# A fused cross-attention and expert FFN kernel: the opening loads cut into other groups, put in another order, and two of them held back

## What is computed

```python
# one layer
qh, kh, vh = heads(layernorm(x) @ wq + bq), heads(ctx @ wk + bk), heads(ctx @ wv + bv)   # 16 heads of 8
out = softmax((qh @ kh^T * 8**-0.5) @ vh, axis=-1)        # softmax over the 8 channels of a head
x = x + concat(out) @ wo.T + bo

t = rmsnorm(layernorm(x)) * norm_w
probs = softmax(t @ gate_w.T); topw, topi = top_k(probs, 2); topw /= sum(topw)
h1 = t @ w1.T + 2 * (t @ a1[e].T) @ b1[e].T               # 8 experts e, rank 16, hidden 512
h3 = t @ w3.T + 2 * (t @ a3[e].T) @ b3[e].T
act = silu(h1) * h3
out_e = act @ w2.T + 2 * (act @ a2[e].T) @ b2[e].T
x = x + sum over the two chosen experts of topw * out_e
```

## Time and profile before

| | us |
|---|---|
| three executions, median (lowest, highest) | 320.5 (319.81, 321.2) |
| the profiled execution's own time | 323.57 |
| its span, from its first to its last instruction | 321.5 |
| PE busy in that span | 303.4 |
| ScalarE, VectorE, GpSimd busy | 198.5, 224.3, 189.4 |

### The profile page before, as it was taken

One profiled execution on the slowest core, in us unless ns is written; L12 is line 12 of the kernel. 1 busy time (PEld: TensorE's weight loads), 2 busy tenths in 40 slices (PEclk: granted clock), 3 DMA queues, 4 the chain that ended last, 5 costly groups with the idle time before them and its releaser, 6 DMA issues. The chain is left out here.

```text
span 321.5 us, 4664 instructions
## 1 busy us (share of the span) xinstructions
PE 303.4 (94%) x1569; PEld 246.1 (77%) x1569; DVE 224.3 (70%) x621; ACT 198.5 (62%) x337; POOL 189.4 (59%) x171
## 2 busy tenths in 40 slices
PE   7577999989999999999999999999999999998994
PEld 6455777768887888878887888888887878786873
DVE  2476985787668956796678955895749945963475
ACT  2146695377774786587665777497746757763531
POOL 3251458945895279817794289718781389326920
PEclk9679899999999999999999999999999999999997
DMA  7502002000200002000200011000000000000000
GB/s 221 205 0 68 0 1 67 0 1 3 65 33 2 0 20 81 0 0 3 65 33 3 0 46 54 0 2 0 1 35 0 1 2 34 1 2 0 33 0 33
DMA packets 4919, 8.95 MB, mean 28 GB/s; under 512 B 544, under 2 KB 1568, under 8 KB 4896
## 3 DMA queue, kind: packets, MB, share of 16 engines
q1 hardware_dynamic: 4176, 7.41, 6.8%
q10 hardware_dynamic: 720, 1.25, 1.3%
HBM read 6.56 MB, written 2.10 MB: 27 GB/s over the span
## 5 line engine op out<-in xcount | busy, mean ns | idle before, releaser
L844 ACT ACTIVATE silu<-h_ps 128x512 f32<-128x512 f32 x64 | 38.2, 597 | 28.1 <-PE h_ps L569 26.2
L569 PE MATMUL h_ps<-um_hi,b_hi 128*128 128x512 f32 x128 | 51.4, 401 | 0.1
L1125 DVE TENSOR_TENSOR act_first<-silu,h_ps 128x512 f32<-128x512 f32 x32 | 21.9, 687 | 42.1 <-ACT silu L844 25.1
L569 PE MATMUL h_ps<-um_lo,b_hi 128*128 128x512 f32 x128 | 50.7, 396 | 0.2 <-DVE um_lo L1223 0.2
L569 PE MATMUL h_ps<-um_hi,b_lo 128*128 128x512 f32 x128 | 50.6, 395 | 0.0
L1348 POOL TENSOR_TENSOR heads<-e_o,rec_o 128x512 f32<-128x512 f32 (+1 forms) x9 | 14.8, 1645 | 47.4 <-DVE rec_o L1034 47.4
L1377 POOL TENSOR_TENSOR scaled<-act_second,ratio 128x512 f32<-128x512 f32 x24 | 31.4, 1309 | 17.0 <-DVE act_second L1125 16.8
L1125 DVE TENSOR_TENSOR act_second<-silu,h_ps 128x512 f32<-128x512 f32 x32 | 21.3, 683 | 14.6 <-PE h_ps L569 13.9
L569 PEld LDWEIGHTS h_ps<-um_lo,b_hi 128*128 128x128 f32 x128 | 24.0, 188 | 6.4 <-DVE um_lo L1223 0.7
L569 PEld LDWEIGHTS h_ps<-um_hi,b_hi 128*128 128x128 f32 x128 | 24.1, 188 | 5.7 <-DVE act_first L1125 0.4
L569 PEld LDWEIGHTS h_ps<-um_hi,b_lo 128*128 128x128 f32 x128 | 24.1, 189 | 5.4
(11 more groups left out here) (273 smaller groups left out, 817.0 us busy)
## 6 DMA issues: line engine op xcount, KB each, us to landing
x_in<-in_x_dram SPq DMA_DIRECT2D x7, 256.0 KB, 2.9
ctx_in<-in_ctx_t_dram SPq DMA_DIRECT2D x7, 256.0 KB, 3.2
out_dram<-y SPq DMA_DIRECT2D x7, 256.0 KB, 2.0
act_second<-in_hidden_w_dram SPq DMA_DIRECT2D x1, 512.0 KB, 10.0
act_second<-in_lora_w_dram ACTq DMA_DIRECT2D x1, 512.0 KB, 10.2
v_parts<-in_down_w_dram SPq DMA_DIRECT2D x1, 512.0 KB, 4.3
attn_sb<-in_attn_w_dram SPq DMA_DIRECT2D x1, 260.5 KB, 4.6
qkv_sb<-in_qkv_w_dram ACTq DMA_DIRECT2D x1, 256.5 KB, 3.6
```

The source lines that it names most:

```text
L569: mm = nc.tensor.matmul((h1_ps, h3_ps)[s][n % 2][:], b13[w][:, s, c * P:(c + 1) * P], um[k][m][:, s, :], start=False, stop=(i == 2), skip_ ...
L844: nc.scalar.activation(silu[:, n % SILU_RING, :], h1_ps[n % 2][:], ACT.Silu).then_inc(silu_done.sem, 1)
L1125: nc.vector.tensor_tensor((act_first, act_second)[k][:, c, :], silu[:, n % SILU_RING, :], h3_ps[n % 2][:], ALU.mult).then_inc(act_done.sem, 1)
```

## The change

The four-part tile `qkv_sb` becomes two: `wkv_sb` (key and value weights, 128 KB) and `query_sb` (query weights, identity and query bias, 128.5 KB), each with a semaphore of its own, so there are seven groups of weights in place of six. The context's first half, `wkv_sb`, the bias row and the context's second half now stand in this order on ACT's queue; `query_sb` goes third on SP's queue, ahead of `attn_sb`. SP waits for the bias row (`rows_in`) before it starts block 1's x and, behind that, `w13_raw`. ACT waits for `attn_sb` (`attn_w_in`) before it starts `b13_raw`. Each reader waits for the semaphore of what it reads. On DVE one pair near the end of the prologue changes places.

```diff
+        wkv_sb = sb("wkv_sb", [P, 2 * P])[:]
+        query_sb = sb("query_sb", [P, 2 * P + 1])
+        wq_sb, ident, bq_sb = query_sb[:, 0:P], query_sb[:, P:2 * P], query_sb[:, 2 * P:]
...
             for i in HALVES:
                 sp.dma_start(flat(x_in[0])[:, cols(i)], x[:, cols(i)]).then_inc(x_first[i], 16)
+            sp.dma_start(query_sb[:], query_w).then_inc(query_w_in, 16)
             sp.dma_start(attn_sb[:], attn_w).then_inc(attn_w_in, 16)
+
+            sp.wait_ge(rows_in, 16)
             load_x(1)
             sp.dma_start(w13_raw, hidden_w).then_inc(hidden_w_in, 16)
...
-            pe.wait_ge(qkv_w_in, 16)
+            pe.wait_ge(wkv_in, 16)
             keys_values_ahead(0, 0)
             keys_values_ahead(0, 1)
+            pe.wait_ge(query_w_in, 16)
             turn_x(0, 0)
...
-            sc.dma_start(qkv_sb[:], qkv_w).then_inc(qkv_w_in, 16)
-            for i in HALVES:
-                sc.dma_start(ctx_in[:, cols(i)], ctx_t[:, cols(i)]).then_inc(ctx_first[i], 16)
+            sc.dma_start(ctx_in[:, cols(0)], ctx_t[:, cols(0)]).then_inc(ctx_first[0], 16)
+            sc.dma_start(wkv_sb, wkv).then_inc(wkv_in, 16)
             sc.dma_start(rows_sb[:], rows.partition_broadcast(P)).then_inc(rows_in, 16)
-            sc.dma_start(b13_raw, lora_w).then_inc(lora_w_in, 16)
-            sc.wait_ge(qkv_w_in, 16)
+            sc.dma_start(ctx_in[:, cols(1)], ctx_t[:, cols(1)]).then_inc(ctx_first[1], 16)
+            sc.wait_ge(wkv_in, 16)
             nc.scalar.copy(wkv_split[0][:], wkv_sb).then_inc(w_hi_ready, 1)
             sc.wait_ge(attn_w_in, 16)
+            sc.dma_start(b13_raw, lora_w).then_inc(lora_w_in, 16)
             nc.scalar.copy(a13[0][:], a13_raw).then_inc(w_hi_ready, 1)
+            sc.wait_ge(query_w_in, 16)
             x_turned(0, 0)
...
-            ve.wait_ge(qkv_w_in, 16)
+            ve.wait_ge(query_w_in, 16)
             nc.vector.tensor_copy(ident_bf[:], ident).then_inc(ident_bf_ready, 1)
...
+            first_normalise(tok, x1[0], mv2, rstd2, rstd2_done, tok_done, 1)
             mask_ktv(1)
-            first_normalise(tok, x1[0], mv2, rstd2, rstd2_done, tok_done, 1)
             ve.wait_ge(nw_ready, 1)
```

More of the change, by code:

```diff
@@ L72, in upto, with build_program @@
     return None if i is WHOLE else i + 1
-def build_program(nc: bass.Bass, x, ctx_t, qkv_w, attn_w, rows, hidden_w, lora_w, down_w, b2, out):
+def build_program(nc: bass.Bass, x, ctx_t, wkv, query_w, attn_w, rows, hidden_w, lora_w, down_w, b2, out):
     with ExitStack() as ctx:
@@ L87, in signal @@
             return Signal(sem(name), per_block, first)
-        qkv_sb = sb("qkv_sb", [P, 4 * P + 1])
-        wkv_sb, wq_sb = qkv_sb[:, 0:2 * P], qkv_sb[:, 2 * P:3 * P]
-        ident, bq_sb = qkv_sb[:, 3 * P:4 * P], qkv_sb[:, 4 * P:4 * P + 1]
+        wkv_sb = sb("wkv_sb", [P, 2 * P])[:]
+        query_sb = sb("query_sb", [P, 2 * P + 1])
+        wq_sb, ident, bq_sb = query_sb[:, 0:P], query_sb[:, P:2 * P], query_sb[:, 2 * P:]
         attn_sb = sb("attn_sb", [P, 2 * P + 1 + EXPERTS + 2 * ER])
@@ L221, in build_program @@
         last_out, last_turned = (odd_ps, h1_ps[0]), (even_ps, h3_ps[0])
-        qkv_w_in = sem("qkv_w_in")
+        wkv_in = sem("wkv_in")
+        query_w_in = sem("query_w_in")
         attn_w_in = sem("attn_w_in")
@@ L1461 @@
         "ctx_t": a["ctx_1024"].transpose(2, 0, 1).reshape(D, BATCH * SEQ),
-        "qkv_w": np.concatenate([heads_side_by_side(at("wk_w")), heads_side_by_side(at("wv_w")),
-                                 heads_side_by_side(at("wq_w")), np.eye(P, dtype=np.float32),
-                                 at("wq_b").reshape(HEADS * DK, 1)], axis=1),
+        "wkv": np.concatenate([heads_side_by_side(at("wk_w")), heads_side_by_side(at("wv_w"))], axis=1),
+        "query_w": np.concatenate([heads_side_by_side(at("wq_w")), np.eye(P, dtype=np.float32),
+                                   at("wq_b").reshape(HEADS * DK, 1)], axis=1),
         "attn_w": np.concatenate([head_mask, at("wo_w").T, ff("norm_w").reshape(D, 1), ff("gate_w").T,
```

## The result

Over 20 executions of each kernel the change has a median of 319.57 us (317.66 to 321.42) and the kernel before 321.62 (319.81 to 324.37): a ratio of 0.9936 with an interval of 0.9914 to 0.9959, or a gain of 2.05 us with one of 1.3 to 2.8. It is faster, by more than 0.5% as it came out, though the interval ends at 0.41%. The forecast was a gain of 3.2 us. The time itself ends 0.2 us above the range of 315.7 to 319.4.

A forecast was written before the change was run, and what follows sets the result against it. The prologue was taken to bound the kernel, its hole ended by the late bias row. Gains of 2.5 us (keys times values) and 0.7 (clock) sum to 3.2: from 320.5 to 317.3 us, range 315.7 to 319.4.

The forecast's parts named there:

- Rival (c): Bias row's load: one DRAM row read 128 times is late by itself, landing at 9.7; 320.0 us, chance 0.16.
- The two next waits: Prologue: PE waits for the context's second half, landing 7.1 us; DVE's moments wait for block 1's x, landing 10.5.
- Rival (d): Block 1's x, started at 6.5, lands at 16.5, past the needed 14.75, delaying DVE's mask; 322.3 us, chance 0.05.
- keys times values, 2.5 us: PE in the prologue: keys times values starts at 8.45 in place of 10.96; gain 2.5 us, bounds 0.6 and 3.1.
- moved at 6.35 by the earlier trace, with 0.7 us behind it: Context's second half, fourth on ACT's queue: 0.594 MB moved at 6.35 us, plus 0.7 us lag, landing at 7.1.
- or within some tenths: Identity in `query_sb`, third on SP: there before DVE reaches it or within some tenths; cost 0.
- the clock term, 0.7 us: PE's chain from 10.96 to 16.85 at 1.2 GHz: 0.7 us gain, bounds 2.35 gain and 0.85 loss.
- The low stretch may therefore start elsewhere: PE's clock: the long hole goes but a shorter one is new, so low clock may move; another stands at 21.2 to 24.6.
- I take 0.7 of gain, nearer the middle of these ends: PE's clock: 0.7 us taken between 2.35 gain with no low stretch and 0.85 loss with an earlier fall.
- The rest of the loads: Held loads, `w13_raw` and block 1's context among them: landed by 12.7 to 14.7 us; cost nothing, at worst 0.3.
- (b): Low clock starts earlier on PE, or block 1's x comes at 12 us: 318.2 to 318.9 us, chance 0.18.
- a low clock before 11 us that lasts as long as the old one: One of the signs in PE's clock that would show the forecast wrong; the old one was 0.50 for 6.6 us.

The follow-up runs named there:

- the run with the filled hole: Kernel before plus 48 unused products on PE in its idle time before the first keys times values: 321.78 us over 12, ratio 0.9978.
- x free with the row stored once and 128 times: Kernel before, block 1's x unheld, hidden and LoRA weights held: 318.95 us, ratio 0.9901; with the bias row 128 times in DRAM: 318.88 us, 0.9893.

## Why the prediction was right in kind and too high in size

**Right: what bounds, and the mechanism.** The prologue decides, and what moves the start of the even stretch moves the end by as much (282.4 us behind it in both kernels). The bias row was late because of what is queued: with the order alone the time got worse, with the waits alone came the whole gain. Rival (c) holds for a part of it, 1.6 of 8.0 us. Once the other loads are held that part is gone too, and with it removed alone, keys times values started as early as in the change.

**Right: what takes the bias row's place.** The two next waits were named: PE's for the context's second half, and DVE's for block 1's x, which caps the gain. Block 1's x landed 3.9 us after its issue (taken: 4.0), started 0.7 us late and made the moments begin at 11.07. Its cap explains why three kernels with an earlier start of keys times values were no faster: with the context's half third it was 7.71, with a bias row stored 128 times ahead of that half 8.01, with the one load of weights second 8.16, and the mask still came at 12.63, 12.97 and 13.24. Rival (d) would have needed a landing at 14.75, and it came at 11.1.

**Wrong in size: keys times values, 2.5 us.** It measured 10.96 - 9.20 = 1.76. The working was: half landed 7.1, then 1.35 us. Measured: 8.01 and 1.19. The failing step is "moved at 6.35 by the earlier trace rows, with 0.7 us behind it", and both parts of it were too short. The earlier trace rows are the pace of another order. In the new one the engines fall behind in the dip from 4.0 to 4.5 us, the bytes are complete near 7.0, and the landing follows 1.0 us later. Why there is a dip, and why the lag was longer, stays open. The bounds of 6.5 to 9.0 held the landing. The bias row, taken at 6.5, came by 7.2, behind the same dip, and the identity ("or within some tenths") made DVE wait 1.77 us, though beside PE's wait and not in front of it. The 1.76 is also the figure of one execution: in the profile with the pair put back, the same opening started keys times values at 9.96, and with the row stored 128 times at 9.09.

**Not borne out: the clock term, 0.7 us.** "The low stretch may therefore start elsewhere" was right; the step that isn't borne out is "I take 0.7 of gain, nearer the middle of these ends", with both ends from one execution. The clocks give 0 by their medians and an estimated 0.4 us by their means. The rule cited there, that idle time brings back the half rate (the Trainium skill, "TensorE: Matmul & The Clock Gate", part 1), would have made it 2.35 us. The profile of the run with the filled hole agrees in that 11 to 17.6 us ran at 1.00, but a low stretch came next, behind 6.6 us in which PE was busy for 4.5, and the gain of that run ends at 1.7 us.

**The sum again** with what was measured: 1.76 us and 0 to 0.4 of the clock are 1.8 to 2.2, against 2.05 with an interval of 1.3 to 2.8. Nothing in it asks for a further term.

**Small terms.** The exchanged pair is worth 0. `attn_sb` landed at 7.8 and not near 7.0; ACT's split of it at 8.19 is off PE's path, as taken. The rest of the loads cost nothing that shows at the end, though PE waits 0.92 us at 14.76 for block 1's context, which was taken to have no wait: it has one now, earlier than its old reader at 17.58.

**The base.** The forecast stood on the median of three, 1.1 us below that of the twenty. With a gain of 2.05 from 320.5 the time would have been 318.45, inside the range. Of the cases, the result then lies in (b), 318.2 to 318.9 from 320.5. Its mechanism isn't in the profile of the change, which has no fall of the clock before 11 us. It is in that of the change with the pair put back: the clock is low from before 8 to 17 us, and the second half's four products take 0.94 us longer (taken: 0.9). That is the sign named for being wrong, "a low clock before 11 us that lasts as long as the old one", and it comes in some executions and not in others. How many of the twenty had it is not known.

**No better version.** Every kernel that holds the bulk loads has a ratio from 0.984 to 0.9964, and most of the intervals overlap. The waits alone in the old order do as well as the whole change. The four kernels with that order (both waits, SP's alone, x free with the row stored once and 128 times) have ratios of 0.9893 to 0.9920, and their 32 executions have a mean clock of 0.9887 against 0.9830 of the kernel before, an estimated 0.9 us. So how the opening is laid out can move the clock; here it did so in the old order more than in the new.

## What to carry to other kernels

When a small load that gates the start is late, look at what is queued beside and behind it before reordering: holding the bulk loads until it has landed gave here all of the gain, while the reordering without holding lost 0.5%. Look at the load itself too: storing the repeated row as an ordinary tile, with nothing held, gave as much over four executions. Then find who waits for the held load, since the gain ends where that wait begins. And compare the granted clock over several executions before a difference of two profiles, or a term for the clock, is believed.

## What the runs showed of the hardware that I had not expected

- Executions of one kernel differ by 3 us and more with the mean granted clock (0.967 to 0.999, 1.55 us per 0.01). In the profiles the difference is in the prologue: behind the start of the even stretch they agree within 0.5 us, but for one.
- The clock column can read 1.00 over an opening in which the same eight products take 3.75 us in one profile and 2.27 in another.
- One DRAM row read into 128 partitions, beside other loads, took 8.0 us (8.0 to 8.1 in three profiles), and 6.4 in one with the row stored 128 times; the load beside it went from 7.9 to 6.2 us. With little beside it: 5.5 and 5.4.
- What is queued behind a load delays its landing: the same 196 KB as last of four took 4.7 us with nothing behind, 5.4 with 512 KB behind on its own queue, and 8.0 with 512 KB there and 768 KB on the other. The Trainium skill, "DMA: Bandwidth & Descriptors", "Anatomy of one DMA", gives 2.0 us plus the bytes at 436 GB/s for a transfer that GpSimd starts; the estimate by that page is 2.5 us for the row by itself. No run here has it by itself: ACT starts it, behind up to 512.5 KB on its queue, and it took 4.7 us or more in every run.
- Two loads with rows of 1 KB followed by the bias row: the DMA engines moved 0.06 MB in half a microsecond, against 0.15 to 0.19 in other orders.
